# TensorE's order written by points: six runs of score pairs a quad, values ahead of a fill in the same gap

## The chip, the cores and the metric

One core of one Trainium2 chip. The metric is the device time of one execution in microseconds (us), as a median of three runs; lower is better.

## The reference

Eight sequences of 512 tokens by 256 channels go through three residual parts. Layer norm is written out in float32 with its own statistics.

```
x = x + 0.5 * ffn(layernorm(x))          # silu(x @ Wg.T) * (x @ Wu.T) @ Wd.T, hidden 768, weights int / 127
x = x + attention(layernorm(x))          # 16 heads of 16 channels
x = x + 0.5 * ffn(layernorm(x))

scores = einsum("bhld,bhsd->bhls", qh, kh) * 0.25 - slope[h] * abs(l - s)
out    = softmax(scores) @ vh ;  out @ Wo.T + bo
```

## The kernel before

The kernel runs in three stages: the first feed-forward block for all eight sequences, the attention for all eight, the second feed-forward block for all eight. The change touches the attention stage alone, so the rest is left out here.

**Quads, steps and points.** A sequence's attention is four *quads* of four heads (n = 0 to 3). A quad has eight *steps* (s = 0 to 7): step s takes key tile kt = s // 2 (128 keys) and one pair of heads, s % 2. A step has two *points* (i = 0, 1), one per head, so a quad has points 0 to 15, point p = 2 * s + i. At every point TensorE makes two matmuls that stand in different halves of its rows and so run side by side; I call them a **pair**:

- `scores(b, n, s, i)` makes the 128 x 512 scores of this quad (printed as `ps<-q_aug,k_aug 62*128`). They go in turn to three PSUM banks (`SCORE_BANKS`), so it waits until the exponential of three points earlier is done (`exp_done`).
- `scores_for_max` makes a tile of scores of a quad 24 tiles ahead (`MAX_LEAD`; printed as `ps<-k_aug,q_aug 60*128`), of which VectorE takes the row maxima (`row_maxima`, line 880). These tiles go in turn to three other banks (`MAX_BANKS`), so it waits until the reduction of three points earlier is done (`s1_used`).

ScalarE takes the exponential of each score bank into `probs` (line 685). GpSimd multiplies the tile on the diagonal by a table (line 553, `fixed`), once per step. When both steps of a key tile are done, `weigh_values` (lines 1199 to 1208) multiplies `probs` with the values: four matmuls into one bank (`ps<-probs,v_aug`), called **values** here. `probs` has two slots by kt, so the exponential of key tile kt waits for the values of kt - 2 (`pv_done`). Values of the quad's first key tile also wait for `heads_t_ready`: ScalarE has copied the result bank of the quad before (`take_heads`, line 669, in step 2).

**Fills.** Other work of TensorE is spread over the steps by the table `FILLS` (lines 117 to 122): five a quad, in steps 1, 3, 4, 5 and 7. They are the projections of the next sequence (`qk`, `v`), its transposes (`xt`), the transposes and output products of heads (`heads`, `turn`, `out`), and in step 4 `max`: the transpose of a quad's row maxima (line 1060), which waits until VectorE has reduced all 16 tiles of that quad, the last of them being the tile of point 7. All use one PSUM bank, so a fill waits until ScalarE has emptied it of the one before (`empty`, lines 618 to 643). After a `heads` fill (step 5) VectorE divides in step 7 (`divide`, lines 933 and 935); after an `xt` fill it splits two steps later (line 925). In quads 1 and 2 it also applies a layer norm in steps 2, 4 and 6 (line 755, `APPLY_AT`).

**The order.** Every engine runs its own program in order; TensorE's is `turn` (lines 1220 to 1245). Within a step it makes the pair of point 2s, then the values (even steps) or the fill (odd steps; in step 4 the fill follows the values), then the pair of point 2s + 1:

```
scores(b, n, s, 0)
...
scores_for_max(b, tiles[:1])
if s % 2 == 0:
...
if tiles:
    scores(b, n, s, 1)
scores_for_max(b, tiles[1:])
```

So a gap with other work stands ahead of every odd point: eight gaps a quad, and between them eight **runs** of two pairs (points 15 and 0, 1 and 2, 3 and 4, and so on). ScalarE's `turn` (lines 671 to 692) empties the fill of a step between that step's two exponentials (`fill_first`), VectorE's `turn` (lines 973 to 990) puts its other work between the step's two reductions.

Of the kernel before, what the change touches and what calls it, by code (L numbers as in the profile page):

```python
# [40 lines left out]
B, L, C = 8, 512, 256  # L41
H, D = 16, 16
FF = 768
TT = L // P
# [3 lines left out]
NQ = H // QH  # L48
STEPS = 2 * TT
# [72 lines left out]
}  # L122
ALL_FILLS = list(FILLS.values())

BANKS_BEFORE = {"qk0_next": 4, "qk1_next": 5, "v0_next": 4, "v1_next": 5, "qk2_next": 4, "qk3_next": 5, "max0_next": 4}
FILLS_BEFORE = list(BANKS_BEFORE)
# [33 lines left out]
def max_tiles_at(b, step):  # L160

    made = MAX_LEAD + 2 * step
    return range(made, min(made + 2, MAX_TILES) if b == B - 1 else made + 2)
# [30 lines left out]
def build_program(nc, d_x, d_wgu, d_wdn, d_watt, d_bo, d_qb, d_kb, d_diag, d_eye, d_scale, d_out):  # L194
    d_qrows = nc.dram_tensor("q_rows_scratch", (2, 2 * NSEG, NP, L), F32).ap()
    d_krows = nc.dram_tensor("k_rows_scratch", (ROWS - ROW_BIAS, L), F32).ap()
    with ExitStack() as ctx:
# [80 lines left out]
        def first(b):  # L278
            return isinstance(b, int) and b == 0
# [292 lines left out]
        def _(act):  # L572
# [45 lines left out]
            def empty(b, name):  # L618

                at = fill_no(b, name)  # L620
                seq, kind, part = fill_parts(b, name)
                bank = bank_of(b, name)
                act.wait_ge(filled, at + 1)
                if kind in STAGED:
                    before = two_before(b, name)
                    if before:
                        wait_done(act, *before)
                    if kind == "qk" and part % 2 == 0:
                        if name == "qk0_next" and b < 0:
                            act.wait_ge(scale_in, 16)  # L630
                        nc.scalar.activation(stage[:, slot_of(b, name), :], bank, ACT.Identity, scale=q_scale[:, 0:1]
                                             ).then_inc(drained, 1)
                    else:
                        nc.scalar.copy(stage[:, slot_of(b, name), :], bank).then_inc(drained, 1)  # L634
                elif kind == "v":
                    if not (isinstance(seq, int) and seq == 0):
                        act.wait_ge(v_ready, NQ * seq)
                    nc.scalar.copy(v_new[:, 2 * part:2 * part + 2, :],
                                   bank.rearrange("p (t c) -> p t c", t=2)).then_inc(drained, 1)
                elif kind == "max":  # L640
                    quad_no = seq * NQ + part
                    wait(act, max_split, quad_no)
                    nc.scalar.copy(max_row[:, :], bank[0:TT * QH, 0:P]).then_inc(drained, 1)
# [27 lines left out]
            def turn(b):  # L671
                for n in range(NQ):
                    for s in range(STEPS):
                        kt, pair = s // 2, s % 2
                        quad_no = b * NQ + n
                        g = quad_no * STEPS + s
                        name = FILLS.get((n, s))
                        name = name if name in fills_of(b) else None
                        fill_first = name and len(max_tiles_at(b, n * STEPS + s)) > 0
                        wait(act, pv_done, quad_no * TT + kt - 1)  # L680
                        for i in range(2):
                            if i == 1 and fill_first:
                                empty(b, name)
                            act.wait_ge(st_done, 2 * g + i + 1)
                            nc.scalar.activation(probs[:, kt % 2, 2 * pair + i, :], score_bank(2 * g + i),  # L685
                                                 ACT.Exp, scale=SLOPE_UNITS[pair]).then_inc(exp_done, 1)
                        if s == 2 and not (first(b) and n == 0):
                            take_heads(quad_no - 1)
                        if name and not fill_first:
                            empty(b, name)  # L690
                        if name:
                            round_hi(b, name)

# [6 lines left out]
        def _(dve):  # L700
# [272 lines left out]
            def turn(b):  # L973
                for n in range(NQ):
                    for s in range(STEPS):
                        tiles = max_tiles_at(b, n * STEPS + s)
                        row_maxima(b, tiles[:1])
                        name = FILLS.get((n, s - DIVIDE_LATER))
                        if name in fills_of(b) and name.startswith(HEADS):
                            divide(b, name)  # L980
                        name = FILLS.get((n, s - SPLIT_LATER))
                        if name in fills_of(b) and name.startswith(SPLIT_DVE):
                            split(b, name)
                        if first(b) and (n, s) in LAST_BLOCKS_AT:
                            last_blocks(LAST_BLOCKS_AT[n, s])
                        if b + 2 < B and (n, s) in APPLY_AT:
                            apply_kept(b + 2, (APPLY_AT[n, s],))
                        if b + 2 == B and (n, s) in FIRST_ROWS_C_AT:
                            first_rows(FIRST_ROWS_C_AT[n, s])
                        row_maxima(b, tiles[1:])  # L990

            turns(dve, turn)
            for tile in range(TT):
# [6 lines left out]
        def _(pe):  # L1000
# [210 lines left out]
            def scores(b, n, s, i):  # L1211
# [5 lines left out]
                matmul(score_bank(no), k_aug[b % 2][rows, 2 * n + pair, kt * P:(kt + 1) * P],  # L1217
                       q_aug[b % 2][rows, 2 * n + pair, :], True, True).then_inc(st_done, 1)

            def turn(b):  # L1220
                for n in range(NQ):
                    for s in range(STEPS):
                        quad_no = b * NQ + n
                        if s == 0:
                            pe.wait_ge(max_moved, (quad_no + 1) * (16 * 2))
                        tiles = max_tiles_at(b, n * STEPS + s)
                        name = FILLS.get((n, s))
                        scores(b, n, s, 0)
                        if not tiles:
                            scores(b, n, s, 1)  # L1230
                        scores_for_max(b, tiles[:1])
                        if s % 2 == 0:
                            if s >= 4:
                                weigh_values(quad_no, n, (s - 4) // 2, b)
                            elif not (first(b) and n == 0):
                                weigh_values(quad_no - 1, (n - 1) % NQ, s // 2 + 2, b)
                            if name in fills_of(b):
                                fill(b, name)
                        elif name in fills_of(b):
                            if first(b) and (n, s) == (0, 1):  # L1240
                                pe.wait_ge(ffn[0]["y_used"], 2 * B)
                            fill(b, name)
                        if tiles:
                            scores(b, n, s, 1)
                        scores_for_max(b, tiles[1:])

            for b in range(B):
                turn(b)
# [34 lines left out]
```

## Time and profile before

| what | value |
|---|---|
| median of three runs | 800.43 us (797.69 to 805.07) |
| profiled execution | 801.11 us, span 799.2 us |
| attention stage in the span | from 188 us to 640 us |
| one sequence in its middle | 56.8 us |
| TensorE busy | 756.9 us (95% of the span) |
| VectorE, ScalarE, GpSimd busy | 623.7, 521.9, 450.1 us |

A busy matmul row includes the time a matmul takes through the array, so rows of neighbours overlap. How fast TensorE advances is read from the distance between starts.

### The profile page before, as it was taken

The numbers are of one execution on the slowest core, as the hardware profiler recorded it, in microseconds if no ns is written. First come the engines' busy times: TensorE is split into PE (matmuls) and PEld (weight loads), VectorE is DVE, ScalarE is ACT, GpSimd is POOL, SyncE is SP. The second block draws the span as 40 slices with busy tenths as digits, with TensorE's granted clock in tenths as the row PEclk, the third lists the DMA queues.
The fourth block names the chain that finished last, engine by engine and source line by source line (L and its number), as shares of the span: only waits on it lengthen the run. The fifth ranks groups of instructions, "written<-read, shape, count | busy, mean of one in ns | idle before, by whom it ended". The sixth has DMA issues, their size and how long they took to land.

```text
span 799.2 us, 13303 instructions
## 1 busy us (share of the span) xinstructions
PE 756.9 (95%) x4576; PEld 466.5 (58%) x4576; DVE 623.7 (78%) x1267; ACT 521.9 (65%) x1001; POOL 450.1 (56%) x550
## 2 busy tenths in 40 slices
PE   2999999999999999999999999999999998999998
PEld 1878887775444454454453444544443486878887
DVE  6798877968899879878978889889888265567763
ACT  5344444336878878879888888888787754434433
POOL 0433355336656866766766766767676545344433
PEclk9999999999999999999999999999999998999999
DMA  9440015501550730722522523615400000000001
GB/s 356 164 64 3 2 29 75 59 2 26 88 74 3 109 53 16 106 41 36 87 41 43 81 41 66 83 17 81 70 13 2 2 3 28 27 30 28 29 29 54
DMA packets 21637, 43.20 MB, mean 54 GB/s; under 512 B 3864, under 2 KB 5928, under 8 KB 21352
## 3 DMA queue, kind: packets, MB, share of 16 engines
q1 hardware_dynamic: 21544, 41.92, 28.4%
q8 instruction: 63, 1.03, 0.6%
q14 instruction: 30, 0.25, 0.1%
HBM read 12.02 MB, written 4.62 MB: 21 GB/s over the span
## 4 chain that ended last, share of the span: by engine, by line
PE 81%; DVE 13%; issue 2%; ACT 2%; POOL 0%; DMA 0%; DVEq 0%; ACTq 0%
PE ps L1002 75%; DVE row_max L880 5%; DVE xnt L925 2%; PE ps L1065 2%; PE ps L1014 2%; DVE hid L811 1%; ACT probs L685 1%; PE ps L1070 1%; PE ps L1060 1%; DVE w_max L891 1%; DVE newton L732 1%; PE ps L1040 1%; DVE x_sb L853 0%; DMA x_sb<-x_in 0%; DVE stats L704 0%
## 5 line engine op out<-in xcount | busy, mean ns | idle before, releaser
L880 DVE TENSOR_REDUCE row_max<-ps 128x1 f32<-128x512 f32 x512 | 326.2, 683 | 54.7 <-PE ps L1002 53.7
L685 ACT ACTIVATE probs<-ps 128x512 f32<-128x512 f32 x512 | 287.6, 608 | 48.2 <-PE ps L1002 46.5
L553 POOL TENSOR_TENSOR probs<-probs,diag 128x256 f32<-128x256 f32 x256 | 189.1, 740 | 123.6 <-ACT probs L685 121.7
L471 POOL TENSOR_TENSOR hid_r<-hid,hid_r 128x512 fp32r<-128x512 f32 x96 | 124.3, 1299 | 182.3 <-ACT hid_r L580 182.0
L1002 PE MATMUL ps<-xnt,wgu_r 128*128 128x512 f32 x768 | 190.2, 401 | 9.2 <-issue 5.7
L1002 PE MATMUL ps<-q_aug,k_aug 62*128 62x512 f32 x512 | 190.4, 447 | 2.9 <-ACT probs L685 2.2
L1002 PE MATMUL ps<-k_aug,q_aug 60*128 60x512 f32 x512 | 190.1, 452 | 1.4 <-DVE row_max L880 0.8
L1002 PEld LDWEIGHTS ps<-xnt,wgu_r 128*128 128x128 f32 x768 | 142.9, 190 | 47.6 <-issue 9.9
L1002 PEld LDWEIGHTS ps<-q_aug,k_aug 62*128 62x128 f32 x512 | 77.4, 185 | 119.8 <-ACT probs L685 96.0
L586 ACT ACTIVATE gated<-ps 128x512 f32<-128x512 f32 x96 | 57.4, 598 | 128.1 <-PE ps L1002 128.1
L1002 PE MATMUL ps<-probs,v_aug 128*32 128x512 f32 x1024 | 136.2, 604 | 0.1
L811 DVE SCALAR_TENSOR_TENSOR hid<-ps,gated 128x512 f32<-128x512 f32 x96 | 66.2, 689 | 54.3 <-PE ps L1002 44.2
L1002 PE MATMUL ps<-wdn_r,hid_r 128*128 128x256 f32 x768 | 99.2, 285 | 4.6 <-ACT stage L634 2.4
L1002 PEld LDWEIGHTS ps<-wdn_r,hid_r 128*128 128x128 f32 x768 | 94.8, 192 | 7.5 <-ACT hid_r L580 3.5
L1002 PEld LDWEIGHTS ps<-k_aug,q_aug 60*128 60x128 f32 x512 | 76.3, 184 | 12.3 <-DVE row_max L880 8.9
L580 ACT CAST hid_r<-hid 128x512 fp32r<-128x512 f32 x96 | 58.9, 614 | 16.5 <-DVE hid L811 16.4
L634 ACT COPY stage<-ps 128x512 f32<-128x512 f32 x96 | 56.9, 592 | 11.7 <-PE ps L1002 10.7
L1002 PE MATMUL ps<-xnt,wqkv 128*128 128x512 f32 x168 | 46.6, 412 | 0.0
L1002 PEld LDWEIGHTS ps<-probs,v_aug 128*32 128x32 f32 x1024 | 20.3, 108 | 44.4 <-issue 36.2
L741 DVE TENSOR_SCALAR xn<-x_sb,mean_var,rstd 128x256 f32<-128x256 f32 x64 | 43.2, 700 | 0.3
L495 POOL TENSOR_TENSOR parts<-stage,parts 128x512 fp32r<-128x512 f32 x32 | 41.2, 1288 | 0.0
L704 DVE BATCH_NORM_STATS2 stats<-x_sb 128x6 f32<-128x256 f32 x96 | 34.1, 410 | 5.4 <-DMA x_sb<-x_in 5.4
(72 smaller groups left out, 656.6 us busy)
## 6 DMA issues: line engine op xcount, KB each, us to landing
q_aug<-parts SPq DMA_DIRECT2D x96, 128.0 KB, 4.6
k_aug<-parts SPq DMA_DIRECT2D x96, 128.0 KB, 4.6
x_sb<-x_in SPq DMA_DIRECT2D x8, 512.0 KB, 12.8
x_out<-x_sb SPq DMA_DIRECT2D x7, 512.0 KB, 2.6
diag<-diag_table SPq DMA_DIRECT2D x1, 2048.0 KB, 19.1
wgu_i<-w_gate_up SPq DMA_DIRECT2D x2, 768.0 KB, 6.1
w_att<-w_att SPq DMA_DIRECT2D x1, 1024.0 KB, 11.4
q_aug<-max_parts SPq DMA_DIRECT2D x64, 8.0 KB
```

What stands on the lines that cost most here:

```text
L471: nc.gpsimd.tensor_tensor(hid_r[:, 1, f, :], hid[:, f % 2, :], hid_r[:, 0, f, :].bitcast(F32), ALU.subtract).then_inc(s["hid_lo"], 1)
L495: nc.gpsimd.tensor_tensor(lo, stage[:, slot_of(b, name), :], hi.bitcast(F32), ALU.subtract).then_inc(done[SPLIT_POOL], 1)
L553: nc.gpsimd.tensor_tensor(tile, tile, diag[:, kt % 2, n * QH + 2 * pair:n * QH + 2 * pair + 2, :], ALU.mult).then_inc(fixed, 1)
L580: nc.scalar.copy(hid_r[:, 0, f, :], hid[:, f % 2, :]).then_inc(s["hid_hi"], 1)
L586: nc.scalar.activation(gated[:, f % 2, :], ps[:, gate_at + f % 2, :], ACT.Silu, scale=DEQ).then_inc(s["gated_ready"], 1)
L634: nc.scalar.copy(stage[:, slot_of(b, name), :], bank).then_inc(drained, 1)
L685: nc.scalar.activation(probs[:, kt % 2, 2 * pair + i, :], score_bank(2 * g + i), ACT.Exp, scale=SLOPE_UNITS[pair]).then_inc(exp_done, 1)
L704: nc.vector.bn_stats(stats[:, slot, tile, :], x_of(b, tile)).then_inc(ln_step, 1)
L741: nc.vector.tensor_scalar(xn[:, tile, :], x_of(b, tile), mean_var[:, 0, tile, 0:1], rstd[:, 0, tile:tile + 1], ALU.subtract, ALU.mult).the ...
L811: nc.vector.scalar_tensor_tensor(hid[:, f % 2, :], ps[:, up_at + f % 2, :], DEQ, gated[:, f % 2, :], ALU.mult, ALU.mult).then_inc(s["hid_r ...
L880: nc.vector.reduce_max(row_max[:, quad % 2, i, pair, t:t + 1], max_bank(b * MAX_TILES + tile), mybir.AxisListType.X).then_inc(s1_used, 1)
L1002: return nc.tensor.matmul(out, lhs, rhs, start=start, stop=stop, **k)
```

## The change

TensorE's `turn` is written by points, from two tables. `VALUES_AT` says ahead of which point which values stand (-2 and -1 are the last two key tiles of the quad before), `FILL_AT` ahead of which point the fill of which step stands. Where both have the same point (3, 8 and 11), values stand first. Other work now stands ahead of points 0, 3, 6, 8, 11 and 14: six gaps, and six runs of 3, 3, 2, 3, 3 and 2 pairs. Values stand one or two points earlier than before (ahead of 0, 3, 8, 11 where they stood ahead of 1, 5, 9, 13). The fills of steps 3, 4 and 7 stand one point earlier. ScalarE empties a fill ahead of the exponential of the point that the fill stands ahead of. VectorE makes both reductions of step 3 ahead of that step's other work.

```diff
+VALUES_AT = {0: -2, 3: -1, 8: 0, 11: 1}
+FILL_AT = {3: 1, 6: 3, 8: 4, 11: 5, 14: 7}
...
-                        fill_first = name and len(max_tiles_at(b, n * STEPS + s)) > 0
                         wait(act, pv_done, quad_no * TT + kt - 1)
                         for i in range(2):
-                            if i == 1 and fill_first:
+                            if name and FILL_AT.get(2 * s + i) == s:
                                 empty(b, name)
...
-                        if name and not fill_first:
-                            empty(b, name)
                         if name:
                             round_hi(b, name)
...
-                        row_maxima(b, tiles[:1])
+                        row_maxima(b, tiles if s == 3 else tiles[:1])
...
-                        row_maxima(b, tiles[1:])
+                        if s != 3:
+                            row_maxima(b, tiles[1:])
...
+            def values_due(b, n, point):
+
+                quad_no, kt = b * NQ + n, VALUES_AT[point]
+                if kt >= 0:
+                    weigh_values(quad_no, n, kt, b)
+                elif not (first(b) and n == 0):
+                    weigh_values(quad_no - 1, (n - 1) % NQ, TT + kt, b)
+
+            def fill_due(b, n, point):
+
+                name = FILLS[n, FILL_AT[point]]
+                if name in fills_of(b):
+                    if first(b) and (n, point) == (0, 3):
+                        pe.wait_ge(ffn[0]["y_used"], 2 * B)
+                    fill(b, name)
+
...
                         tiles = max_tiles_at(b, n * STEPS + s)
-                        name = FILLS.get((n, s))
-                        scores(b, n, s, 0)
-                        if not tiles:
-                            scores(b, n, s, 1)
-                        scores_for_max(b, tiles[:1])
-                        if s % 2 == 0:
-                            if s >= 4:
-                                weigh_values(quad_no, n, (s - 4) // 2, b)
-                            elif not (first(b) and n == 0):
-                                weigh_values(quad_no - 1, (n - 1) % NQ, s // 2 + 2, b)
-                            if name in fills_of(b):
-                                fill(b, name)
-                        elif name in fills_of(b):
-                            if first(b) and (n, s) == (0, 1):
-                                pe.wait_ge(ffn[0]["y_used"], 2 * B)
-                            fill(b, name)
-                        if tiles:
-                            scores(b, n, s, 1)
-                        scores_for_max(b, tiles[1:])
+                        for i in range(2):
+                            point = 2 * s + i
+                            if point in VALUES_AT:
+                                values_due(b, n, point)
+                            if point in FILL_AT:
+                                fill_due(b, n, point)
+                            if point == 0:
+                                pe.wait_ge(max_moved, (b * NQ + n + 1) * (16 * 2))
+                            scores(b, n, s, i)
+                            scores_for_max(b, tiles[i:i + 1])
```

TensorE at the end of the second sequence's second quad, before: a `qk` fill (`xnt,wqkv`) stands ahead of point 15; then come the pairs of points 15 and 0, values, and the pairs of points 1 and 2. The pair of point 14 stands ahead of the fill and is not in these rows.

```order
L1002 MATMUL ps<-xnt,wqkv 128x512 x5
L1002 MATMUL ps<-q_aug_61,k_aug_85 128x512 [waits exp_done]
L1002 MATMUL ps<-k_aug_85,q_aug_61 128x512 [waits s1_used]
L1002 MATMUL ps<-q_aug_61,k_aug_85 128x512 [waits exp_done,max_moved]
L1002 MATMUL ps<-k_aug_85,q_aug_61 128x512 [waits s1_used]
L1002 MATMUL ps<-probs,v_aug 32x512 [waits fixed]
L1002 MATMUL ps<-probs,v_aug 32x512 x3
L1002 MATMUL ps<-q_aug_61,k_aug_85 128x512 [waits exp_done]
L1002 MATMUL ps<-k_aug_85,q_aug_61 128x512 [waits s1_used]
L1002 MATMUL ps<-q_aug_61,k_aug_85 128x512 [waits exp_done]
L1002 MATMUL ps<-k_aug_85,q_aug_61 128x512 [waits s1_used]
```

The same place now, behind the same fill: the pairs of points 14 and 15, values, then the pairs of points 0, 1 and 2.

```order
L1002 MATMUL ps<-q_aug_61,k_aug_85 128x512 [waits exp_done]
L1002 MATMUL ps<-k_aug_85,q_aug_61 128x512 [waits s1_used]
L1002 MATMUL ps<-q_aug_61,k_aug_85 128x512 [waits exp_done]
L1002 MATMUL ps<-k_aug_85,q_aug_61 128x512 [waits s1_used]
L1002 MATMUL ps<-probs,v_aug 32x512 [waits fixed]
L1002 MATMUL ps<-probs,v_aug 32x512 x3
L1002 MATMUL ps<-q_aug_61,k_aug_85 128x512 [waits exp_done,max_moved]
L1002 MATMUL ps<-k_aug_85,q_aug_61 128x512 [waits s1_used]
L1002 MATMUL ps<-q_aug_61,k_aug_85 128x512 [waits exp_done]
L1002 MATMUL ps<-k_aug_85,q_aug_61 128x512 [waits s1_used]
L1002 MATMUL ps<-q_aug_61,k_aug_85 128x512 [waits exp_done]
L1002 MATMUL ps<-k_aug_85,q_aug_61 128x512 [waits s1_used]
```

Point 14 has moved from ahead of the fill to behind it, values have moved from behind point 0 to ahead of it, and the run behind them has three pairs instead of two.

VectorE in the first quad of a sequence, before: two splits of an `xt` fill (`xnt<-stage,xnt`), in steps 3 and 5, stand between reductions, and the reciprocal and the product of `divide` stand in step 7.

```order
L880 TENSOR_REDUCE row_max<-ps 128x1 [waits s1_done] x8
L925 TENSOR_TENSOR xnt<-stage,xnt 128x512 [waits split_hi]
L880 TENSOR_REDUCE row_max<-ps 128x1 [waits s1_done] x4
L925 TENSOR_TENSOR xnt<-stage,xnt 128x512 [waits split_hi]
L880 TENSOR_REDUCE row_max<-ps 128x1 [waits s1_done] x4
L933 RECIPROCAL den<-stage 128x16 [waits drained]
L935 TENSOR_TENSOR heads<-stage,den 128x4x64 [waits den_ready]
```

The same rows now (the lines have other numbers in the changed file):

```order
L879 TENSOR_REDUCE row_max<-ps 128x1 [waits s1_done] x9
L924 TENSOR_TENSOR xnt<-stage,xnt 128x512 [waits split_hi]
L879 TENSOR_REDUCE row_max<-ps 128x1 [waits s1_done] x3
L924 TENSOR_TENSOR xnt<-stage,xnt 128x512 [waits split_hi]
L879 TENSOR_REDUCE row_max<-ps 128x1 [waits s1_done] x4
L932 RECIPROCAL den<-stage 128x16 [waits drained]
L934 TENSOR_TENSOR heads<-stage,den 128x4x64 [waits den_ready]
```

One reduction, that of point 7, has moved ahead of the first split. Nothing else has moved on VectorE: the divide still stands between the reductions of points 14 and 15.

## Rows read from the trace of the kernel before

**Rows 1.** Windows, one sequence: us; busy PE, PEld, DVE, ACT, POOL; PEclk; DMA
```profile
330.49:387.25 56.76, 56.27 (x367) 26.22 (x366) 48.53 (x80) 47.92 (x97) 40.41 (x57) 1.00 0.40 58
```
**Rows 2.** Timeline of PE (start us, us, engine, line, operation): two pairs, then values
```profile
330.49 0.49 PE L1002 MATMUL ps<-q_aug,k_aug 62*128 62x512 f32 x1
331.15 1.06 PE L1002 MATMUL ps<-probs,v_aug 128*32 128x512 f32 x8
332.15 0.49 PE L1002 MATMUL ps<-q_aug,k_aug 62*128 62x512 f32 x1
```
**Rows 3.** Timeline of PE, last sequence, no maxima: one pair of scores, then values
```profile
621.28 0.50 PE L1002 MATMUL ps<-q_aug,k_aug 62*128 62x512 f32 x2
621.71 1.06 PE L1002 MATMUL ps<-probs,v_aug 128*32 128x512 f32 x8
```
**Rows 4.** Timeline of PE at the start of the attention: three pairs in one run
```profile
188.06 0.50 PE L1002 MATMUL ps<-q_aug,k_aug 62*128 62x512 f32 x1
...
188.40 0.63 PE L1002 MATMUL ps<-q_aug,k_aug 62*128 62x512 f32 x2
188.64 0.40 PE L1002 MATMUL ps<-k_aug,q_aug 60*128 60x512 f32 x1
```
**Rows 5.** Timeline of PE: values, then the transpose of the row maxima
```profile
335.09 1.06 PE L1002 MATMUL ps<-probs,v_aug 128*32 128x512 f32 x8
336.09 0.28 PE L1060 MATMUL ps<-eye,row_max 128*16 128x128 f32 x1
```
**Rows 6.** Timeline of DVE around the divide, two quads
```profile
339.82 1.29 DVE L880 TENSOR_REDUCE row_max<-ps 128x1 f32<-128x512 f32 x2 [0.38 <-PE ps L1002]
341.03 0.24 DVE L933 RECIPROCAL den<-stage 128x16 f32<-128x16 f32 x1
341.31 0.96 DVE L935 TENSOR_TENSOR heads<-stage,den 128x256 f32<-128x256 f32 x1
342.19 1.28 DVE L880 TENSOR_REDUCE row_max<-ps 128x1 f32<-128x512 f32 x2
...
384.77 0.42 DVE L935 TENSOR_TENSOR heads<-stage,den 128x256 f32<-128x256 f32 x1
385.11 3.33 DVE L880 TENSOR_REDUCE row_max<-ps 128x1 f32<-128x512 f32 x5
```
**Rows 7.** Timeline of PE: the pair ahead of the first of these reductions
```profile
339.25 0.50 PE L1002 MATMUL ps<-q_aug,k_aug 62*128 62x512 f32 x1
```
**Rows 8.** Timeline of PE, first quad of a sequence: its two waits for DVE
```profile
364.40 0.27 PE L1060 MATMUL ps<-eye,row_max 128*16 128x128 f32 x1 [0.41 <-DVE row_max L880]
...
367.57 0.49 PE L1002 MATMUL ps<-q_aug,k_aug 62*128 62x512 f32 x1
...
368.38 0.50 PE L1002 MATMUL ps<-k_aug,q_aug 60*128 60x512 f32 x1
368.80 1.66 PE L1002 MATMUL ps<-xnt,wqkv 128*128 128x512 f32 x6
```
**Rows 9.** Timeline of POOL beside the two divides
```profile
341.25 0.73 POOL L534 TENSOR_TENSOR x_sb<-x_sb,bo 128x256 f32<-128x256 f32 x1
385.63 0.74 POOL L553 TENSOR_TENSOR probs<-probs,diag 128x256 f32<-128x256 f32 x1 [1.57 <-ACT probs L685]
```
**Rows 10.** Timeline of DVE: the reduction that the transpose at 364.40 waited for
```profile
363.57 1.28 DVE L880 TENSOR_REDUCE row_max<-ps 128x1 f32<-128x512 f32 x2
```
**Rows 11.** Timeline of PE: an xt fill and the pair behind it
```profile
358.77 0.66 PE L1040 MATMUL ps<-eye,xn 128*128 128x128 f32 x4
359.36 0.49 PE L1002 MATMUL ps<-q_aug,k_aug 62*128 62x512 f32 x1
```
**Rows 12.** Timeline of ACT: an exponential behind values; from emptying an xt fill to take_heads
```profile
336.22 0.60 ACT L685 ACTIVATE probs<-ps 128x512 f32<-128x512 f32 x1 [0.60 <-PE ps L1002]
...
359.70 0.61 ACT L634 COPY stage<-ps 128x512 f32<-128x512 f32 x1
...
362.12 0.65 ACT L669 COPY heads_t<-ps 128x512 f32<-128x512 f32 x1
```

More of the change, by code:

```diff
@@ L1222, in turn @@
                     for s in range(STEPS):
-                        quad_no = b * NQ + n
-                        if s == 0:
-                            pe.wait_ge(max_moved, (quad_no + 1) * (16 * 2))
                         tiles = max_tiles_at(b, n * STEPS + s)
-                        name = FILLS.get((n, s))
-                        scores(b, n, s, 0)
-                        if not tiles:
-                            scores(b, n, s, 1)
-                        scores_for_max(b, tiles[:1])
-                        if s % 2 == 0:
-                            if s >= 4:
-                                weigh_values(quad_no, n, (s - 4) // 2, b)
-                            elif not (first(b) and n == 0):
-                                weigh_values(quad_no - 1, (n - 1) % NQ, s // 2 + 2, b)
-                            if name in fills_of(b):
-                                fill(b, name)
-                        elif name in fills_of(b):
-                            if first(b) and (n, s) == (0, 1):
-                                pe.wait_ge(ffn[0]["y_used"], 2 * B)
-                            fill(b, name)
-                        if tiles:
-                            scores(b, n, s, 1)
-                        scores_for_max(b, tiles[1:])
+                        for i in range(2):
[8 more added lines that the diff above has]
+                            scores_for_max(b, tiles[i:i + 1])
             for b in range(B):
```

## The prediction

> **What bounds the kernel now.** I read the windows by sequence first, then TensorE's timeline for one sequence, then VectorE's, ScalarE's and GpSimd's beside it, and last the waits. In a middle sequence TensorE is busy 56.27 of 56.76 us at full granted clock; VectorE 48.53, ScalarE 47.92, GpSimd 40.41 [rows 1]. So TensorE sets the pace, but two engines stand at 84 to 86%, and what TensorE is spared is worth something only where their results are already there when it comes earlier. I count in starts on TensorE, since its busy rows overlap.
>
> **The saving: two runs fewer.** A run of two pairs takes 0.66 us from its first start to the values behind it (330.49 to 331.15) [rows 2]; one pair alone takes 0.43 (621.28 to 621.71) [rows 3]. So a further pair costs 0.23, and each run some 0.20 on top. In the one run of three that waits for nothing, the second pair starts 0.34 and the third a further 0.24 behind (188.06, 188.40, 188.64) [rows 4]; with the 0.32 that the last pair of a run takes (0.66 - 0.34), three pairs take 0.34 + 0.24 + 0.32 = 0.90. A quad had 8 x 0.66 = 5.28; it gets 4 x 0.90 + 2 x 0.66 = 4.92. **Saved: 0.36 a quad, 1.44 a sequence.**
>
> The Trainium skill would have none of this: its page "TensorE: Matmul & The Clock Gate", section "Step-by-step: what each phase is for", says that weights of the next matmul are pulled ahead of a running one where they go to other rows or to the spare weight buffer. By that rule a boundary between runs is hidden and two fewer save nothing. The 0.20 a run says otherwise here, so I use 1.44 and keep the rule as a rival.
>
> Values with a fill right behind them are new in two gaps a quad (points 3 and 11). Values take 1.00 with a pair behind them (331.15 to 332.15) [rows 2] and 1.00 with the max transpose behind them (335.09 to 336.09) [rows 5]. I take no change; a fill there could gain or lose up to the 0.20 of a boundary, 2 x 4 x 0.20 = 1.6 a sequence either way, which goes into the range.
>
> **The cost, first place: the third pair behind point 15.** The row maxima have three banks, so the tile of point 2 needs the reduction of point 15 done. Before, point 14 stood ahead of a long fill, and its reduction and the divide ran beside that fill. Now 14 and 15 both stand behind it. Count from the start of pair 14. TensorE, unhindered: pair 15 at 0.34, values 0.66, pair 0 at 1.66, pair 1 at 2.00, pair 2 at 2.23, values 2.55. VectorE: it starts a reduction 0.56 after the start of the first pair of a run (339.82 [rows 6] behind 339.25 or 339.26 [rows 7]); two reductions take 1.21 until the reciprocal starts (339.82 to 341.03), so one some 0.61; reciprocal 0.28 (to 341.31); the product 0.88 until the next reduction (341.31 to 342.19), or 0.34 in another quad (384.77 to 385.11) [rows 6]. So reduction 15 starts at 0.56 + 0.61 + 0.28 + 0.34 to 0.88 = 1.79 to 2.33, takes 0.67 (two take 1.28) [rows 6], and a tile starts 0.06 or so later: 2.52 to 3.06. A pair whose tile waited is followed 0.42 after that tile (368.38 to 368.80) [rows 8], so values come at 2.94 to 3.48 instead of 2.55: **0.39 to 0.93 late.** Which end? In the slow divide GpSimd ran an addition at 341.25; in the quick one it began nothing until 385.63 [rows 9]. Now the divide falls where GpSimd has mostly finished step 6 and waits for step 7, so I go below the middle and take 0.60, 2.40 a sequence.
>
> On that difference the Trainium skill's page "SBUF — State Buffer", section "SBUF: two separate sides", has a rule: GpSimd and a VectorE operation with two SBUF inputs lock a shared port, and the later one blocks until the other ends. The rows agree in direction (0.42 against 0.96 busy, with GpSimd's 0.73 beside it). By it, every quad in which GpSimd still works there is at the long end, which is the third rival below.
>
> **Second place: the max transpose ahead of point 8.** It needs reduction 7. Before, pair 8 and values stood between; now values alone. From the start of pair 6, behind its fill: pair 7 at 0.34, values 0.66, transpose 1.66. Reduction 6 starts at 0.56, reduction 7 at 0.56 + 0.66 (five take 3.33 us: (3.33 - 0.67) / 4) [rows 6] = 1.22, and the transpose comes 0.83 after the start of the reduction it needs (363.57 [rows 10], 364.40 [rows 8]): 2.05. **0.39 late**, in quads 1 to 3: 1.17 a sequence. VectorE's new order (both reductions of step 3 first) keeps this from being worse in the first quad, and costs nothing itself.
>
> **Third place: the first quad.** Its fills at points 3 and 6 are short `xt` transposes (358.77 to 359.36, 0.59) [rows 11], so ScalarE doesn't catch up. From the end of the fill at point 3, TensorE unhindered: three pairs 0.90, fill 0.59, pairs 6 and 7 0.66, values at 2.15. These need `take_heads`, which in ScalarE's order comes behind: emptying the fill, exponential 3, rounding, exponentials 4 and 5. From the start of emptying (359.70) to the end of that copy (362.12 + 0.65) are 3.07 us [rows 12]; with some 0.15 at both ends 3.2. **1.07 late**, once a sequence; the max transpose hides in it. The price of the earlier place of values is thus a wait for ScalarE.
>
> Other edits cost nothing of their own: emptying a fill one exponential earlier is the same work in ScalarE (47.92 of 56.76), POOL and SP keep their order, and row maxima go to their DMAs one point sooner.
>
> **The sum.** New waits a sequence: 2.40 + 1.17 + 1.07 = 4.64. Gone: the first quad's waits before, 0.41 at 364.40, and the run from 367.57 that took 1.23 to the fill instead of 0.66, 0.57 [rows 8]; 0.98 together. Spared: 1.44. Net 4.64 - 0.98 - 1.44 = **+2.22 a sequence**. Six sequences are full: +13.3. The first lacks five fills, two values and one divide; the last has no maxima in its final quad and a half, and its scores wait for exponentials, where earlier values may gain a little. I set these two together at nothing, between -3 and +4. Against the profiled execution's 801.11 us (span 799.2) that is 814.4; this run lies 0.7 above the median of 800.43. **Forecast 814**, 1.7% slower. A measurement of this kernel tells apart about 1% (8 us).
>
> **Rivals.**
> 1. *Earlier values release ScalarE (faster).* The exponential of point 8 began 0.60 late because its `probs` slot was held by values that TensorE had put behind scores 8 [rows 12]; the same holds at every new key tile. With values ahead, ScalarE and then GpSimd and the banks run ahead, and all waits vanish, the old ones too: 801.1 - 6 x (1.44 + 0.98) = 787. It decides if TensorE's waits in the middle stay under 1.44 a sequence. Against it: TensorE's busy share leaves only half a microsecond for it [rows 1], and the bank of point 15 hangs on VectorE, which this does not help.
> 2. *Short ends (no change).* Each divide takes the short end (0.39), the max transpose waits half (0.20), the first quad half (0.55): 1.56 + 0.60 + 0.55 = 2.71, net 2.71 - 2.42 = +0.29, so 803.
> 3. *Long ends (slower still).* Divides at 0.93: 3.72 + 1.17 + 1.07 - 2.42 = +3.54 a sequence, 822. For it: two of the four divides were slow where GpSimd worked beside them.
> 4. *A boundary between runs costs nothing* (the skill's rule above): +2.22 + 1.44 = 3.66, 823. Against it: 0.43 for one pair and 0.66 for two [rows 2, 3].
>
> **How the numbers follow.** Forecast 0.55, rival 1 0.08, rival 2 0.22, rivals 3 and 4 together 0.15 (rival 4 alone 0.03). Faster by over 1%: 0.08. Within 1%: 0.22. Slower by over 1%: 0.55 + 0.15 = 0.70. The range reaches from a little under rival 2 (values and fill at the good end by part of their 1.6 a sequence) to a little over rivals 3 and 4: 799 to 826; rival 1 and the far ends stay out.
>
> **What would show it.** Right: a middle sequence takes some 59 us; the third pair's tile (60-row matmul) of point 2 starts 0.3 to 0.8 behind its scores in every quad, released by VectorE's row maxima; the max transpose shows a wait for row maxima in most quads; values ahead of point 8 wait for `heads_t` in first quads; runs without waits take 0.90 for three pairs. Wrong: sequences at or under 56.8 us, with third pairs that start 0.24 behind the second, or TensorE waiting for GpSimd's `fixed` ahead of points 3 and 11, which I take to be in time.

## The result and the profile after

The changed kernel takes 822.26 us (median of four runs, 818.85 to 825.61) against 800.32 (797.69 to 805.07) for the kernel before, timed beside it: ratio 1.0267, 95% interval 1.0193 to 1.0342. That lies inside the predicted range, 8 us above the forecast of 814. The profiled execution took 825.28 us, span 823.4, so 24.2 us of span are to be found against the 799.2 before.

The windows of a middle sequence, from the max transpose of one of its quads to that of the same quad in the next (columns as in [rows 1]):

```profile
391.72:451.50 59.78, 57.18 (x364) 27.66 (x365) 47.24 (x78) 48.09 (x98) 40.02 (x56) 1.00 0.36 55
```

59.78 us (the next sequence 59.76) against 56.76 in [rows 1]: 3.0 more a sequence, where the forecast had 2.22. VectorE, ScalarE and GpSimd do the same work; TensorE waits for it. I go through the four places where it waits, the three I had forecast first.

**First place, the third pair behind point 15.** TensorE in one quad, and VectorE around the divide in a quad of the next sequence:

```profile
354.86 0.50 PE L1002 MATMUL ps<-q_aug,k_aug 62*128 62x512 f32 x1
...
355.44 0.39 PE L1002 MATMUL ps<-q_aug,k_aug 62*128 62x512 f32 x1
355.74 0.50 PE L1002 MATMUL ps<-k_aug,q_aug 60*128 60x512 f32 x1
356.17 1.06 PE L1002 MATMUL ps<-probs,v_aug 128*32 128x512 f32 x8
```

```profile
400.23 0.42 DVE L934 TENSOR_TENSOR heads<-stage,den 128x256 f32<-128x256 f32 x1
400.57 1.88 DVE L879 TENSOR_REDUCE row_max<-ps 128x1 f32<-128x512 f32 x3
```

The third tile (60 rows) starts 0.30 behind its scores, and the run takes 1.31 to its values instead of 0.90: 0.41 late, in all four quads. The divide takes 0.34 to the next reduction, that of point 15 at 400.57, and the tile that needs it starts at 401.31, 0.74 behind, where I had 0.67 + 0.06. That is the short end of my bounds (0.39), where the two divides in [rows 6] had given one long and one short.

**Second place, the max transpose ahead of point 8:**

```profile
361.94 1.07 PE L1002 MATMUL ps<-probs,v_aug 128*32 128x512 f32 x8
363.29 0.27 PE L1060 MATMUL ps<-eye,row_max 128*16 128x128 f32 x1 [0.28 <-DVE row_max L879]
```

From values to transpose are 1.35 instead of 1.00: 0.35 late (0.39 forecast). In quads 1 and 2 some 0.14 of it stands ahead of the values, but three quads of four lose the 0.35.

**Third place, the first quad:**

```profile
375.26 0.50 PE L1002 MATMUL ps<-q_aug,k_aug 62*128 62x512 f32 x1 [0.27 <-ACT probs L686]
...
376.31 1.06 PE L1002 MATMUL ps<-probs,v_aug 128*32 128x512 f32 x8 [0.55 <-ACT heads_t L671]
377.31 0.28 PE L1060 MATMUL ps<-eye,row_max 128*16 128x128 f32 x1
```

The pair of point 6 starts at 374.49, and its values, 0.66 behind it when nothing waits, come at 376.31: 1.16 late (1.07 forecast), with `take_heads` the last thing waited for. The transpose behind them waits for nothing: hidden, as forecast. The run of three pairs behind it then takes 1.07 to its values (377.52 to 378.59), 0.17 more, which I had not.

**The place I had not seen: quad 1, step 6.** TensorE, VectorE and GpSimd in the same few us:

```profile
333.55 0.50 PE L1002 MATMUL ps<-q_aug,k_aug 62*128 62x512 f32 x1
...
335.30 0.50 PE L1002 MATMUL ps<-k_aug,q_aug 60*128 60x512 f32 x1 [1.01 <-DVE row_max L879]
...
336.32 2.39 PE L1002 MATMUL ps<-xnt,wqkv 128*128 128x512 f32 x6
```

```profile
331.64 0.69 DVE L879 TENSOR_REDUCE row_max<-ps 128x1 f32<-128x512 f32 x1 [0.91 <-PE ps L1002]
332.25 2.40 DVE L754 TENSOR_SCALAR xn<-x_sb,kept_mean,kept_rstd 128x256 f32<-128x256 f32 x1
334.56 2.47 DVE L879 TENSOR_REDUCE row_max<-ps 128x1 f32<-128x512 f32 x4
```

```profile
331.08 0.73 POOL L555 TENSOR_TENSOR probs<-probs,diag 128x256 f32<-128x256 f32 x1 [0.70 <-ACT probs L686]
331.76 0.28 POOL L514 CAST max_parts<-max_row 16x128 fp32r<-16x128 f32 x1
332.12 0.45 POOL L516 TENSOR_TENSOR max_parts<-max_row,max_parts 16x128 fp32r<-16x128 f32 x1
332.54 1.26 POOL L497 TENSOR_TENSOR parts<-stage,parts 128x512 fp32r<-128x512 f32 x1
333.77 0.72 POOL L555 TENSOR_TENSOR probs<-probs,diag 128x256 f32<-128x256 f32 x1
334.82 0.73 POOL L555 TENSOR_TENSOR probs<-probs,diag 128x256 f32<-128x256 f32 x1 [0.33 <-ACT probs L686]
```

VectorE applies a layer norm (line 754) between the reductions of points 8 and 9. It takes 2.40 us, and ends at 334.65, 0.16 behind a chain of GpSimd operations that has no gap over 0.1 (to 334.49). Reduction 9 and those after it are late, and the tile of point 12 waits 1.01 for its bank: the run of three pairs takes 2.77 (333.55 to 336.32) instead of 0.90, **1.87 lost**. In the kernel before, the same apply in the same quad began while `fixed` ran and ended in a hole of GpSimd's work, from 379.20 to 379.79 (timelines of VectorE and GpSimd, before):

```profile
378.98 0.40 DVE L755 TENSOR_SCALAR xn<-x_sb,kept_mean,kept_rstd 128x256 f32<-128x256 f32 x1
```

```profile
378.47 0.73 POOL L553 TENSOR_TENSOR probs<-probs,diag 128x256 f32<-128x256 f32 x1 [0.93 <-ACT probs L685]
379.79 0.28 POOL L512 CAST max_parts<-max_row 16x128 fp32r<-16x128 f32 x1 [0.59 <-ACT max_row L643]
```

Why did the hole go? The chain's first link is the split of the row maxima, which needs ScalarE's copy of the max transpose. Before, GpSimd waited 0.59 for that copy. Now the transpose stands ahead of point 8, the copy is there sooner, and the split follows `fixed` at once. The apply has moved as well: it stands behind reduction 8, and TensorE now makes pair 8 behind values and transpose. Counted from the start of `fixed`, the split came at 1.32 and now comes at 0.68, and the apply came at 0.51 and now comes at 1.17.

**The clock.** The fill behind that wait takes 2.39 us in the rows above, 1.66 in [rows 8]. Windows behind it, and around another one, the clock in the third column from the end:

```profile
330.00:340.00 10.00, 8.86 (x47) 4.02 (x43) 7.81 (x11) 6.54 (x15) 5.17 (x8) 0.85 0.75 105
337.00:340.00 3.00, 3.00 (x13) 1.49 (x15) 1.72 (x4) 1.21 (x3) 0.47 (x1) 0.50 1.08 127
...
510.00:520.00 10.00, 8.76 (x47) 3.88 (x51) 8.21 (x11) 6.94 (x15) 5.59 (x9) 0.89 0.78 109
```

Behind the wait TensorE runs for some us at the lower of its two levels, 1.2 of 2.4 GHz (a granted clock of 0.50 in the second row). From the max transpose of quad 1 to that of quad 2 are 17.2 to 17.4 us where this happens, 16.1 where it doesn't, so one drop costs 1.1 to 1.3. All five sequences in the middle have the blocked apply, and in three of them the clock falls (behind waits of 1.01 to 1.05); in the two others (the sequence of the window at the top is one) it stays at 1.00 behind waits of 1.04 and 1.01. So whether it falls does not follow from the length of the wait alone. The four runs of the changed kernel come in two pairs, near 819 us at a mean granted clock of 0.994 and near 825 at 0.985 and 0.990.

**The 24.2 us.** Five sequences (255.38 to 557.81 us, 250.87 to 534.66 before) take 18.6 more: 5 x 3.0 and three drops of 1.2. What lies ahead of them takes 4.5 more: 2.7 of it in the first sequence where a divide of 1.44 us beside GpSimd holds a tile for 1.52, with a fourth drop behind it, and 1.1 where that sequence's own apply takes 2.19 and holds a tile for 0.81. The seventh sequence takes 1.2 more (59.39 to 60.55), the rest 0.1 less.

### The profile page after: what moved, and what is told of

Its sections match the earlier page's. It is cut to its first block, busy times and chain, and to the rows that moved or that the text cites. A ratio compares the mean times of both kernels' runs of the same rounds, so it can differ in the third digit from the quotient of the medians.

```text
span 823.4 us, 13216 instructions
## 1 busy us (share of the span) xinstructions
PE 763.5 (93%) x4576; PEld 479.1 (58%) x4576; DVE 620.7 (75%) x1267; ACT 523.4 (64%) x1001; POOL 447.9 (54%) x550
## 3 DMA queue, kind: packets, MB, share of 16 engines
q8 instruction: 63, 1.03, 0.6%
## 4 chain that ended last, share of the span: by engine, by line
PE 77%; DVE 15%; issue 3%; ACT 3%; POOL 2%; DMA 0%; DVEq 0%; ACTq 0%; POOLq 0%
PE ps L1002 70%; DVE row_max L879 7%; DVE xn L754 2%; PE ps L1065 2%; PE ps L1014 2%; ACT probs L686 2%; DVE hid L810 1%; PE ps L1070 1%; POOL probs L555 1%; PE ps L1040 1%; PE ps L1060 1%; DVE heads L934 1%; DVE w_max L890 1%; ACT heads_t L671 1%; DVE newton L731 0%
## 5 line engine op out<-in xcount | busy, mean ns | idle before, releaser
L686 ACT ACTIVATE probs<-ps 128x512 f32<-128x512 f32 x512 | 275.7, 606 | 22.1 <-PE ps L1002 19.5
L1002 PE MATMUL ps<-k_aug,q_aug 60*128 60x512 f32 x512 | 186.0, 451 | 10.9 <-DVE row_max L879 10.7
L1002 PE MATMUL ps<-q_aug,k_aug 62*128 62x512 f32 x512 | 175.9, 439 | 4.6 <-ACT probs L686 4.6
L1002 PEld LDWEIGHTS ps<-q_aug,k_aug 62*128 62x128 f32 x512 | 82.0, 187 | 76.3 <-issue 40.8
L1002 PEld LDWEIGHTS ps<-k_aug,q_aug 60*128 60x128 f32 x512 | 81.3, 187 | 33.1 <-DVE row_max L879 29.0
L1002 PE MATMUL ps<-xnt,wqkv 128*128 128x512 f32 x168 | 48.6, 427 | 0.3 <-DVE xnt L924 0.3
L1002 PEld LDWEIGHTS ps<-xnt,wqkv 128*128 128x128 f32 x168 | 30.3, 193 | 14.7 <-ACT stage L636 6.9
```

Of the source, the lines that this page charges most:

```text
L1002: return nc.tensor.matmul(out, lhs, rhs, start=start, stop=stop, **k)
```

## The experiments

That GpSimd's work holds up an operation of VectorE (the lock) is called L where an expectation names theories by letter. Each edit is against the changed kernel unless it is said otherwise; every ratio is against the kernel before, timed in the same runs.

**1. The apply one step earlier.** Its old place is between reductions 8 and 9; step 3 is ahead of GpSimd's chain.

```diff
-APPLY_AT = {(1, 2): 0, (1, 4): 1, (1, 6): 2, (2, 2): 3}
+APPLY_AT = {(1, 2): 0, (1, 3): 1, (1, 6): 2, (2, 2): 3}
```

> Theory L (lock): in the changed kernel the layer-norm apply in step 4 of quad 1 takes 2.40 us instead of 0.40, because GpSimd runs its rounding of maxima, a split and two products back to back beside it; VectorE is 2 us late and TensorE's tile of point 12 waits 1.0. With that apply in step 3, where VectorE idles some 0.9, it takes 0.4 to 0.7, the wait at point 12 goes, the run of 11 to 13 in quad 1 falls from 2.8 to 0.9 us, a sequence from 59.8 to 57.9, the time by 11 us and by what the lower clock behind that wait cost: some 807 to 812. Theory W (work): VectorE is late because runs of three ask for reductions faster than it makes them; the place of one apply changes nothing: 819 to 825.

Measured: 811.49 us (809.12 to 812.88), ratio 1.014 (1.0093 to 1.0187). Windows of a middle sequence, and VectorE's timeline with the apply in it:

```profile
311.58:369.48 57.90, 56.31 (x369) 27.40 (x365) 45.05 (x78) 48.00 (x97) 40.04 (x56) 1.00 0.38 57
```

```profile
325.74 0.40 DVE L754 TENSOR_SCALAR xn<-x_sb,kept_mean,kept_rstd 128x256 f32<-128x256 f32 x1
```

57.90 instead of 59.78: 1.88 a sequence, what that run had lost (1.87). The three clock drops behind it are gone too; the one in the first sequence stays, as its cause (the divide) does. Half of the slowdown (10.8 of 21.9 us) is this one instruction of a sequence.

**2. Both reductions of step 7 ahead of the divide**, so that point 2 need not wait behind it.

```diff
-row_maxima(b, tiles if s == 3 else tiles[:1])
+row_maxima(b, tiles if s in (3, 7) else tiles[:1])
...
-if s != 3:
+if s not in (3, 7):
```

> Both reductions of step 7 ahead of the divide. Theory L, with the prediction's first place: the wait of point 2's tile (0.31, values 0.42 late, four times a sequence) goes, the rest stays: 1.7 us a sequence, some 11 us, 809 to 813. Theory W: the divide is only pushed behind, and the same wait shows at points 2 or 4: under 3 us gained.

Measured: 810.41 us (804.05 to 811.98), ratio 1.0127 (1.0078 to 1.0177). The run of points 0, 1 and 2 in one quad, TensorE and then VectorE:

```profile
318.02 0.50 PE L1002 MATMUL ps<-q_aug,k_aug 62*128 62x512 f32 x1
...
318.36 0.62 PE L1002 MATMUL ps<-q_aug,k_aug 62*128 62x512 f32 x2
318.59 0.39 PE L1002 MATMUL ps<-k_aug,q_aug 60*128 60x512 f32 x1
319.05 0.64 PE L1002 MATMUL ps<-probs,v_aug 128*32 128x512 f32 x4
```

```profile
318.40 0.87 DVE L934 TENSOR_TENSOR heads<-stage,den 128x256 f32<-128x256 f32 x1
```

The third tile starts 0.23 behind the second and waits for nothing, though the divide is a long one (0.87). Values come 1.03 behind the run's start; in the four quads of a sequence it is 1.03, 1.02, 0.93 and 0.95 where the changed kernel had 1.30 to 1.31. So 1.3 of the first place's 1.64 a sequence are undone, and the reciprocal and the product are hidden again. The 0.13 that is left in two quads is another wait: the values come 0.06 behind the end of GpSimd's `fixed` (318.99), which the prediction took to be in time.

**3. Both edits together.**

> Both edits. Theory L: they add, a sequence takes 56.2 us, 798 to 801, about the kernel before. Theory W: no more than 3 us better than the better one of the two alone.

Measured: 796.24 us (792.9 to 798.39, ten runs), ratio 0.9939 (0.9907 to 0.9971); a middle sequence 56.70. The two gains add: 59.78 - 56.70 is 3.1, of which the first gave 1.9 and the second 1.3; the 56.2 expected had counted 1.7 for the second. TensorE's new order is then level with the old one in a middle sequence (56.76) and a little better over the whole; what made it slow was where VectorE's other work stood in it.

**4. `take_heads` earlier as well**: on top of the third, ScalarE copies the result bank ahead of emptying the fill of point 3, in step 1 instead of step 2.

```diff
+if (s, i) == (1, 1) and not (first(b) and n == 0):
+    take_heads(quad_no - 1)
...
-if s == 2 and not (first(b) and n == 0):
-    take_heads(quad_no - 1)
```

> Both edits, and ScalarE's copy of the result bank ahead of emptying the fill of point 3 instead of behind exponential 5. By the prediction's third place values ahead of point 8 in the first quad are 1.16 us late, about 0.5 of it this copy; quads 1 and 2 have 0.12 each: 0.7 a sequence, 4 to 5 us less than both edits alone, 793 to 797. Rival: the score of point 7 waits 0.43 for exponential 4 in any case and the copy is not what ends last: under 1.5 us less.

Measured: 791.81 us (790.35 to 793.22), ratio **0.9894** (0.9849 to 0.994): better than both kernels, and by a little more than expected. In the first quad the wait for `take_heads` is gone; pair 7 still waits for exponential 4, as the rival had said, and of 1.13 late 0.63 are left. Quads 1 and 2 gain nothing, since the transpose waits longer there instead. What is left besides is the second place, 0.35 in three quads (windows of a sequence, then TensorE's timeline):

```profile
361.77:417.97 56.20, 54.84 (x365) 27.03 (x365) 47.13 (x79) 48.46 (x97) 40.73 (x56) 1.00 0.39 58
```

```profile
403.46 1.07 PE L1002 MATMUL ps<-probs,v_aug 128*32 128x512 f32 x8
404.81 0.27 PE L1060 MATMUL ps<-eye,row_max 128*16 128x128 f32 x1 [0.28 <-DVE row_max L879]
...
416.42 0.49 PE L1002 MATMUL ps<-q_aug,k_aug 62*128 62x512 f32 x1 [0.24 <-ACT probs L688]
```

**5. The kernel before, with VectorE's new order in step 3 alone.**

> The kernel before with VectorE's order of step 3 alone changed (both reductions first). The max transpose of first quads waits 0.41 there because the split stands ahead of reduction 7; it should wait no more: 0.41 in seven sequences, some 3 us, 797 to 799. Rival: the split then ends later, and the same time is lost where its fill or the tile of point 14 waits: no change in the time, and the wait moves.

Measured: 798.88 us (793.27 to 806.1, ten runs), ratio 0.9982 (0.995 to 1.0015): inconclusive in time. In the middle sequences the first quad's waits of [rows 8], 0.98, go, but the `heads` fill behind the transpose now waits 0.44 to 0.47 for ScalarE's copy of the maxima: a part of the wait moves, as the rival had it, and a sequence takes 56.24. The seventh sequence gives the gain of five back (62.18 us, 59.39 before). Windows, and the timelines of VectorE and TensorE:

```profile
418.92:475.16 56.24, 55.80 (x368) 25.96 (x365) 47.83 (x79) 47.86 (x97) 40.51 (x56) 1.00 0.40 58
...
560.00:581.00 21.00, 18.53 (x106) 9.24 (x104) 16.78 (x30) 12.04 (x24) 9.47 (x14) 0.84 0.34 49
```

```profile
561.53 2.35 DVE L734 SCALAR_TENSOR_TENSOR rstd<-newton,rstd 128x4 f32<-128x4 f32 x1
```

```profile
420.31 0.66 PE L1066 MATMUL ps<-eye,heads_t 128*128 128x128 f32 x4 [0.44 <-ACT max_row L643]
...
564.54 0.79 PE L1003 MATMUL ps<-k_aug,q_aug 60*128 60x512 f32 x1 [2.47 <-DVE row_max L880]
```

An operation on 128 x 4 numbers, 0.16 us elsewhere, takes 2.35, beside GpSimd operations that follow each other from 561.00 to 563.86; TensorE waits 2.47 and the clock falls.

**6. The changed kernel with VectorE's old order in step 3.**

```diff
-row_maxima(b, tiles if s == 3 else tiles[:1])
+row_maxima(b, tiles[:1])
...
-if s != 3:
-    row_maxima(b, tiles[1:])
+row_maxima(b, tiles[1:])
```

> The changed kernel with VectorE's old order in step 3. In its first quads the max transpose stands behind values that are 1.16 us late by ScalarE, so reduction 7 behind the split ends about when the transpose could start: at most 0.2 a sequence, 819 to 827. If the reductions' order carried the changed kernel, it would lose 0.4 to 0.8 a sequence, 3 to 6 us, and the transpose would show a wait for row maxima of 0.4 or more in first quads.

Measured: 836.13 us (832.53 to 837.54), ratio 1.0443 (1.0388 to 1.0498): a miss, well above what I expected. The sign that I had named for the other case is there, a wait of 0.41 in first quads, with more than twice its 3 to 6 us. I had looked at middle sequences alone. In the first and the seventh sequence VectorE's work of step 3 is a string of layer-norm operations, and with the old order reduction 7 stands behind all of it: transposes wait 1.58, 1.76, 1.44 and 2.62 there. TensorE's timeline, a middle sequence's transpose and the worst, and a window of a middle sequence:

```profile
379.12 0.27 PE L1059 MATMUL ps<-eye,row_max 128*16 128x128 f32 x1 [0.41 <-DVE row_max L879]
...
596.39 0.27 PE L1059 MATMUL ps<-eye,row_max 128*16 128x128 f32 x1 [2.62 <-DVE row_max L879]
```

```profile
400.00:410.67 10.67, 10.47 (x65) 4.99 (x63) 7.93 (x15) 8.25 (x16) 6.63 (x8) 0.88 0.67 93
```

The clock falls in nearly every sequence, too. So the third part of the change, which I had called free, is worth 14 us by the medians (836.13 - 822.26, and 7 between the two profiled executions) beside the other two.

**7. A shorter operation in GpSimd's chain.** The split of `qk1` (line 497) writes 8 of 512 columns; that part's low half is left out, everything else stays in its place.

```diff
-nc.gpsimd.tensor_tensor(lo, ...)
+w = 8 if b >= 0 and name == "qk1_next" else L
+nc.gpsimd.tensor_tensor(lo[:, 0:w], ...)
```

> The changed kernel with GpSimd's split of the fill qk1 cut from 512 columns to 8 (the low part of those keys is left out). Theory L: nothing is moved on VectorE, but GpSimd's row beside the apply of step 4 in quad 1 is 1.2 us shorter; the apply falls from 2.40 to 1.2 or so, the wait at point 12 from 1.0 to under 0.2, and a sequence from 59.8 to about 58.5. Theory W, which knows VectorE's amount of work alone: the apply and the wait stay as they are.

Measured: 811.33 us (810.11 to 813.0), ratio 1.0133 (1.0079 to 1.0187). The apply on VectorE and what GpSimd did beside it:

```profile
384.92 0.49 DVE L755 TENSOR_SCALAR xn<-x_sb,kept_mean,kept_rstd 128x256 f32<-128x256 f32 x1
```

```profile
384.81 0.45 POOL L517 TENSOR_TENSOR max_parts<-max_row,max_parts 16x128 fp32r<-16x128 f32 x1
385.22 0.24 POOL L498 TENSOR_TENSOR parts<-stage,parts 128x8 fp32r<-128x8 f32 x1
385.44 0.73 POOL L556 TENSOR_TENSOR probs<-probs,diag 128x256 f32<-128x256 f32 x1
```

VectorE's program is untouched, and its apply takes 0.49 instead of 2.40 (0.42 to 0.51 in the six sequences that have it); the run behind it takes 0.91 instead of 2.77, a sequence 57.9, and the time is that of the first experiment. So what stretched the apply was GpSimd's work beside it, which is theory L. It also shows that company alone does not do it: here two operations of GpSimd run beside the apply, and it loses 0.09.

**8. The fourth, with the max transpose at point 11**, ahead of the values there, so that reduction 7 has time.

```diff
-FILL_AT = {3: 1, 6: 3, 8: 4, 11: 5, 14: 7}
+FILL_AT = {3: 1, 6: 3, 11: 5, 14: 7}
...
+if point == 11 and FILLS[n, 4] in fills_of(b):
+    fill(b, FILLS[n, 4])
```

ScalarE empties the transpose's bank ahead of exponential 11.

> The version with both edits and the early copy, and the max transpose moved from behind values at point 8 to ahead of values at point 11, with the heads fill behind them. The transpose is 0.35 late at point 8 in all four quads; at point 11 reduction 7 is long done and the heads fill's bank is emptied beside values: 1.4 a sequence, some 9 us less than 791.8, 782 to 786. Rival: the row maxima then come late to the queries, point 0 waits for their DMAs, or GpSimd, which waits for the emptied transpose ahead of its product of step 4, makes values ahead of point 0 late: no gain or a loss.

Measured: 810.34 us (804.37 to 812.97), ratio 1.0107 (1.0058 to 1.0155): a miss of 25 us. No transpose waits any more, but GpSimd's split of the maxima hangs on the transpose, and with it the whole chain behind it moves, now beside the divide (VectorE's and GpSimd's timelines):

```profile
419.86 2.92 DVE L936 TENSOR_TENSOR heads<-stage,den 128x256 f32<-128x256 f32 x1
```

```profile
420.54 1.27 POOL L506 TENSOR_TENSOR x_sb<-stage,x_sb 128x512 f32<-128x512 f32 x1
421.77 0.72 POOL L555 TENSOR_TENSOR probs<-probs,diag 128x256 f32<-128x256 f32 x1
```

GpSimd has no gap over 0.1 from 414.72 to 422.49; the divide takes 2.92 and ends 0.29 behind the chain, and TensorE's run of three pairs beside it takes 2.84 instead of 0.90. It is the changed kernel's own loss once more, at another place.

**9. The fourth, with the max transpose at point 9** (`8: 4` becomes `9: 4`): one pair of time for reduction 7, and one more boundary between runs.

> The fourth experiment's kernel with the max transpose one point later, ahead of point 9 instead of point 8: the tile of point 7 gets one more pair of time before TensorE asks for its reduction, at the price of one more boundary between runs (a pair of point 8 alone, then two pairs). Theory: the transposes lose their wait of some 0.27 in all four quads and each quad pays 0.20 for the boundary: 4 x 0.07 = 0.3 us a sequence less, about 789 to 791 us, a middle sequence at some 55.8; so by itself the change trades a wait for a boundary at nearly the same price. Rival (a boundary costs nothing): 4 x 0.27 = 1.1 us a sequence less, some 785 us. Rival (GpSimd's chain is tied to the transpose, as in the eighth experiment): its pieces move some 0.5 us later and one VectorE operation, a divide or an apply, takes over 1.5 us; TensorE waits 0.5 or more for row maxima there, and the time is 793 us or more.

Measured: 791.85 us (787.76 to 794.26), ratio 0.9891 (0.9861 to 0.9922): level with the fourth. A middle sequence takes 55.98 against 56.17 as a mean of five, 0.2 less, close to the 0.3 expected of a boundary that costs 0.20. TensorE around the transpose:

```profile
388.11 0.49 PE L1002 MATMUL ps<-q_aug,k_aug 62*128 62x512 f32 x1
...
388.54 0.28 PE L1060 MATMUL ps<-eye,row_max 128*16 128x128 f32 x1
388.75 0.49 PE L1002 MATMUL ps<-q_aug,k_aug 62*128 62x512 f32 x1
...
389.42 1.06 PE L1002 MATMUL ps<-probs,v_aug 128*32 128x512 f32 x8
```

One pair 0.43, then two pairs 0.67, so 1.10 for three pairs in two runs; in one run they take 0.90. The transpose waits for nothing: 0.35 in three quads and 0.12 in the first are gone, 1.2 a sequence. It has been paid for with the boundaries, 0.7, and in the first quad a fill is 0.26 late. Free boundaries would have given 1.1 by the rival's count.

## Why the prediction was right in time, and where it was not

Per middle sequence, in us, the terms in the order of the prediction:

| term | forecast | measured | how |
|---|---|---|---|
| two runs fewer | -1.44 | -1.6 | unhindered runs take 0.89 and 0.66, 0.66 before |
| waits of before that go | -0.98 | -1.18 | also 0.05 behind each of four max transposes |
| first place | +2.40 | +1.64 | 4 x 0.41 |
| second place | +1.17 | +1.05 | 3 x 0.35 |
| third place | +1.07 | +1.33 | 1.16 and the run behind it 0.17 |
| blocked apply | none | +1.87 | goes in the first experiment |
| sum | +2.22 | +3.11 | 59.78 - 56.76 = 3.02 by the windows |

**The saving** was right, and with it the row that spoke against rival 4; the ninth experiment shows the 0.20 of a boundary again, in another place. The rule that the next weights are pulled ahead (the Trainium skill, "TensorE: Matmul & The Clock Gate", section "Step-by-step: what each phase is for") does not make a boundary free in this mix of pairs and full fills. That it would was my inference: that section of the Trainium skill speaks of the loading of weights alone.

**The first place** was the right mechanism (the second experiment moves the divide and the tile's wait is gone), mis-sized: 1.64 instead of 2.40, since every divide took the short end. I had argued that GpSimd mostly stands still there, and still taken 0.60 between the ends; by my own argument the short row was the nearer.

**The second and third place** came within 0.12 and 0.26.

**The step that failed** is "Other edits cost nothing of their own", with "row maxima go to their DMAs one point sooner". That sentence followed the transpose only as far as its DMA. Between the two stands GpSimd's split, first of a chain. Its coming 0.64 sooner, and the apply's coming 0.66 later, put the chain beside an apply: 1.87 a sequence that the sum had at nothing. The seventh experiment shows that it was the chain: 2.40 against 0.49 with one GpSimd operation cut from 1.26 to 0.24 us and VectorE's program the same.

I had the rule for it in the text (the Trainium skill, "SBUF — State Buffer", section "SBUF: two separate sides": the later of the two engines blocks until the other ends) and used it only for the divide. The seventh experiment agrees with it in direction. But the apply outlasted three GpSimd operations, where the rule names one. The rule is for VectorE operations with two SBUF inputs or in a two-port mode, and no run here shows whether the apply, which reads one tensor and two columns of scalars, is one of them.

**"It costs nothing itself"**, of VectorE's order in step 3, was right as far as it went and too small: without that edit the changed kernel takes 14 us more.

**The ends** of the attention stage were set at nothing, between -3 and +4; the stretch ahead of the five sequences took +4.5, of which 2.7 lie around one divide beside GpSimd and the drop behind it. The seventh sequence, one of the six that I counted as full, took 1.2 more instead of 2.2. **The drops** of the clock (four; the three in the middle 1.1 to 1.3 each) were in no term.

That the time lies in the range is thus in part luck. Two errors of opposite sign met: the first place was forecast 0.76 a sequence too high, and the apply's 1.87 was missing.

**The rivals.** Rival 1 fell: TensorE's waits grew. Rival 2 had the ends of the first place right, but not the other two: the three places that I had seen took 4.02, nearer to the forecast's 4.64 than to its 2.71, and with the apply cured the kernel takes 811.49, nearer to 814 than to its 803. Rival 3 names 822, the measured time, but its mechanism, a lock on every divide, is not there in the middle sequences: divides were short in all four quads, and the lock sat on the apply. A time that fits is no evidence for its mechanism.

What stays open: which single operation of the chain held the apply, why other applies beside a chain lost less (below), and why two waits of 1.01 and 1.04 left the clock alone when others of the same length did not.

## What to carry to other kernels

When a step of one engine is moved, follow its result through every engine that uses it until something stands still: here transpose, copy, split, and then a whole chain that landed beside an operation of VectorE. Look for the holes in GpSimd's timeline that VectorE's operations stand in, and treat them as part of the schedule. And once an order of TensorE has changed, the old places of the small work (apply, divide, copy of a result) are guesses again: three such moves turned 2.7% slower into 1.1% faster.

## What the runs showed of the hardware that was not expected

- A VectorE operation beside a chain of GpSimd without gaps can take many times its own length: 0.40 became 2.40 (apply), 0.42 became 2.92 (divide, eighth experiment), and 0.16 became 2.35 for 128 x 4 numbers (fifth), too few for a lower rate alone. In these places it outlasted several GpSimd operations in a row, not one. It does not always: in the kernel before, the applies of one sequence took 0.64, 0.40, 1.24 and 0.87, all beside GpSimd, and the first of them (375.07) ended 0.16 behind the first of two operations that follow each other without a gap. TensorE waited for none of these four; the price of a stretched operation is that of the bank that hangs on it.
- One wait of some 1.0 to 1.5 us of TensorE was at times followed by the lower clock, 0.85 and 0.89 over 10 us in the windows, at a price of 1.1 to 1.3 us on top of the wait itself; other waits of the same length were not.
